# Hints on the back edges of the attention loops, a wait ahead of the mask chain, and a new order at the block boundary of the expert stage

## What is computed

```python
xn = layernorm(x)
# attention, 16 heads of 16 features
q = (xn @ Wq.T + bq) * SCALE;  k = xn @ Wk.T + bk;  v = xn @ Wv.T + bv
att = softmax(q @ k.T) @ v @ Wo.T + bo
# experts: 16, each takes the S/2 tokens of each batch with the highest route
scores = softmax(xn @ wg + bg);  mask = one_hot(top_k(scores, 2)).sum(-2)
route = scores * mask / ((scores * mask).sum(0) + EPS_GATE) * 4
seq_ids = top_k(route per expert, S // 2)
h = gelu(xn[seq_ids] @ w1 + b1);  z = xn;  z[seq_ids] += h @ w2 + b2
ffn = layernorm(z) * gamma + beta
out = x + att + ffn
```

## Time and profile before

| | us |
| --- | --- |
| median of 3 runs | 3733.28 |
| lowest and highest | 3726.79, 3736.49 |
| the profiled execution | 3726.04 |
| its span, first to last instruction | 3724.30 |
| `attend` in it, first to last matmul | 257.2 to 3160.9 |
| `finish` in it, from its first matmul | 3187.8 to 3724.3 |

### The profile page before, as it was taken

One profiled execution on the slowest core, in us unless ns is written; L12 is line 12 of the kernel. 1 busy time (PEld: TensorE's weight loads), 2 busy tenths in 40 slices (PEclk: granted clock), 3 DMA queues, 4 the chain that ended last, 5 costly groups with the idle time before them and its releaser, 6 DMA issues. The chain is left out here.

```text
span 3724.3 us, 69317 instructions
## 1 busy us (share of the span) xinstructions
PE 3461.2 (93%) x19888; PEld 1687.1 (45%) x19888; DVE 2971.2 (80%) x2989; ACT 2481.7 (67%) x4783; POOL 926.3 (25%) x1306
## 2 busy tenths in 40 slices
PE   7869999999999999999999999999999999688887
PEld 6424443443443443443434434434434442577776
DVE  7428888888887887888888888888878881578777
ACT  3534777777777777777777777777777774333332
POOL 2640111111221211111111111111212210355555
PEclk9977999999999999999999999999999995799999
DMA  3661111111111111111111111111111110322222
GB/s 100 202 184 34 45 41 41 41 46 41 50 45 40 45 41 41 41 45 40 47 47 43 44 41 41 41 41 47 48 38 48 45 32 10 99 88 81 82 85 76
DMA packets 101400, 213.01 MB, mean 57 GB/s; under 512 B 11393, under 2 KB 59585, under 8 KB 88833
## 3 DMA queue, kind: packets, MB, share of 16 engines
q1 hardware_dynamic: 98576, 207.68, 18.4%
q10 hardware_dynamic: 2544, 1.62, 0.2%
HBM read 148.42 MB, written 59.77 MB: 56 GB/s over the span
## 5 line engine op out<-in xcount | busy, mean ns | idle before, releaser
L791 DVE TENSOR_REDUCE half_max<-m_ps 128x1 f32<-128x1024 f32 x2048 | 2414.0, 1219 | 497.8 <-PE m_ps L709 488.9
L656 ACT ACTIVATE prob<-s_ps 128x512 f32<-128x512 f32 x4096 | 2132.0, 602 | 688.2 <-PE s_ps L725 670.0
L725 PE MATMUL s_ps<-q_feat,k_feat 50*128 50x512 f32 x4096 | 1528.9, 455 | 38.1 <-issue 30.5
L709 PE MATMUL m_ps<-k_feat,q_feat 48*128 48x512 f32 x4096 | 1381.7, 453 | 40.3 <-DMA k_feat<-k_parts 29.3
L725 PEld LDWEIGHTS s_ps<-q_feat,k_feat 50*128 50x128 f32 x4096 | 698.9, 189 | 1294.3 <-ACT prob L656 1094.9
L734 PE MATMUL a_ps<-prob,v_head 128*32 128x512 f32 x8192 | 1130.4, 625 | 31.5 <-issue 31.5
L709 PEld LDWEIGHTS m_ps<-k_feat,q_feat 48*128 48x128 f32 x4096 | 635.6, 191 | 144.8 <-DVE half_max L791 62.6
L549 POOL TENSOR_TENSOR shift<-row_max,shift 128x16 fp32r<-128x16 f32 x64 | 18.0, 281 | 1363.7 <-ACT shift L661 1363.7
L734 PEld LDWEIGHTS a_ps<-prob,v_head 128*32 128x32 f32 x8192 | 165.1, 109 | 287.2 <-issue 229.8
L1074 ACT ACTIVATE g_hi<-g 128x512 fp32r<-128x512 f32 x128 | 80.9, 632 | 257.1 <-DVE g L1115 256.1
L1247 POOL TENSOR_TENSOR g_lo<-g,g_hi 128x512 fp32r<-128x512 f32 x128 | 183.9, 1437 | 218.1 <-ACT g_hi L1074 218.1
(11 more groups left out here) (141 smaller groups left out, 2114.7 us busy)
## 6 DMA issues: line engine op xcount, KB each, us to landing
q_feat<-q_parts SPq DMA_DIRECT2D x128, 256.0 KB
k_feat<-k_parts SPq DMA_DIRECT2D x128, 256.0 KB
q_parts<-parts SPq DMA_DIRECT2D x32, 512.0 KB, 4.8
k_parts<-parts SPq DMA_DIRECT2D x32, 512.0 KB, 4.8
q_feat<-q_parts SPq DMA_DIRECT2D x128, 128.0 KB
k_feat<-k_parts SPq DMA_DIRECT2D x128, 128.0 KB
att_dram<-att SPq DMA_DIRECT2D x64, 256.0 KB, 15.9
mask_bc<-mask_b SPq DMA_DIRECT2D x128, 128.0 KB, 3.3
```

Of the source, the lines that this page charges most:

```text
L656: act.activation(prob[tile(r, kt) % R][:, qb * BLK:(qb + 1) * BLK], s_ps[slot(r, kt, qb, turn) % R][:, :], ACT.Exp).then_inc(exped, 1)
L709: ins = pe.matmul(m_ps[p % 2][:, k * BLK:(k + 1) * BLK], q_feat[r % 2][LOW, qt * P:(qt + 1) * P], k_feat[r % 2][LOW, key:key + BLK], start ...
L725: pe.matmul(s_ps[slot(r, kt, qb, turn) % R][:, :], k_feat[r % 2][UP, kt * P:(kt + 1) * P], q_feat[r % 2][UP, qb * BLK:(qb + 1) * BLK], sta ...
L791: dve.tensor_reduce(half_max[r][:, p // 2, p % 2:p % 2 + 1], m_ps[p % 2][:, :], AX.X, ALU.max).then_inc(maxed, 1)
```

## The change

Three edits. In `attend` all five loops get `hint_back_edge=True`. In `attend` DVE waits for the last head's `split_shift` before the mask chain. In `finish` PE's `project` moves ahead of the first `unhide` of a block, and DVE's addition of the shift (`shift_x`) moves from the end of a block to behind the statistics in the next one.

```diff
-            with pool.Fori(0, ROUNDS) as i:
+            with nc.Fori(0, ROUNDS, engines=[ENGINE.Pool], hint_back_edge=True) as i:
...
-            with sp.Fori(0, ROUNDS) as i:
+            with nc.Fori(0, ROUNDS, engines=[ENGINE.SP], hint_back_edge=True) as i:
...
-            with act.Fori(0, ROUNDS) as i:
+            with nc.Fori(0, ROUNDS, engines=[ENGINE.Activation], hint_back_edge=True) as i:
...
-            with pe.Fori(0, ROUNDS) as i:
+            with nc.Fori(0, ROUNDS, engines=[ENGINE.PE], hint_back_edge=True) as i:
...
-            with dve.Fori(1, HEADS // R) as i:
+            with nc.Fori(1, HEADS // R, engines=[ENGINE.DVE], hint_back_edge=True) as i:
...
             dve.wait_ge(search, (TOP + 1) * BIT - 1)
+            dve.wait_ge(shift_done, HEADS)
             dve.wait_ge(v_ready, HEADS)
...
-                    unhide(blk, u, e)
                     if last and e == 0:
                         project(blk - 1)
+                    unhide(blk, u, e)
...
                 ins.then_inc(renormed, 1)
+
+            def shift_x(blk):
                 dve.wait_ge(renormed, blk + 1)
-
                 dve.tensor_tensor(x_in[:, :, :], x_in[:, :, :], shift_bc[:, :].unsqueeze(1).broadcast_to([P, TPB, D]),
                                   ALU.add).then_inc(shifted, 1)
...
             def add_sum(blk):
+                dve.wait_ge(renormed, blk + 1)
                 for k in range(TPB):
...
                         add_sum(blk - 1)
                         statistics(blk - 1)
+                        shift_x(blk - 1)
```

More of the change, by code:

```diff
@@ L31 @@
 ds = bass.ds
+ENGINE = mybir.EngineType
 P = 128
@@ L1216, in _ @@
             statistics(NBLK - 1)
+            shift_x(NBLK - 1)
             scale(NBLK - 1)
```

## The result

| | before | after |
| --- | --- | --- |
| median (lowest to highest) of 4 runs each, us | 3734.89 (3726.79 to 3737.26) | 3624.80 (3613.66 to 3637.90) |
| the profiled execution; its span | 3726.04; 3724.30 | 3633.97; 3632.2 |
| granted clock over the span | 0.947 | 0.969 |

The granted clock is that of TensorE, as a share of its full speed. The ratio is 0.971, with an interval of 0.967 to 0.975: 110 us less between the medians, 92.1 between the two spans. The page after, first part, answers rows 1; the second line is the clock in tenths over 40 slices of the span, where the 6 is the last head.

The account below looks back on a forecast made before the run. PE, busy 93% of the span, was taken as the bound, losing time in stops and at low clock. Gains of 73.4 + 3.7 + 8 = 85.1 us off 3726.04 gave 3641 us, range 3606 to 3664.

Parts of the forecast that it names:

- both engines must be freed: At the attention loop's back edges, PE and ACT both lose instruction fetch time, ACT's loss ending last; hinting both gains 73.4 us.
- The 0.43 us for a hinted edge: Cost assumed for each hinted back edge in attend, taken from DVE's short-bodied loop; nine make 3.9 us.
- the 8.6: Price in us of each unhinted back edge in attend, from transpose distances; nine cost 77.3 us.
- Rival 3: Back edges in attend: the hint does nothing, only 3.7 + 8 us come, 3715 us; chance 0.07.
- Rival 2: Back edges in attend: only one of the two engines profits, half the price stays, 3678 us; chance 0.07.
- rival 4: A case in which the kernel is not faster, given a chance of 0.04; its details are not in the text.
- The mask wait: At the last head's shift, PE's stop goes because DVE now waits before the mask chain; gain 3.7 us.
- No way back up: In the last head, a fallen clock does not recover, as 77 us at 0.50 with PE full show.
- rival 1: Last head of attend: the clock stays up throughout, gaining 27 us more, 3614 us; chance 0.39.
- `finish`: At its block boundaries, PE's waits only move and split; the clock falls less often, gaining 8 us of a possible 12.9.
- the lock: In finish, POOL's num_lo holds DVE's neighbouring operation; shortening over 20 us would say it does not catch the gate.
- then the shift takes its free 1.22: In finish, after statistics 1.1 us earlier, the moved shift takes 1.22 us, leaving gate 2 unmoved within 0.1.

## Why the prediction came out

**What bounds the kernel, and both engines must be freed: right.** That ACT's stop ends last was read from rows 3, and the runs with one hint show it: nothing for PE alone, 15 us for ACT alone. The gain at the nine edges was 73.6 against 73.4 predicted.

**That the two numbers agree so closely is luck.** The 0.43 us for a hinted edge were taken from DVE's row, and 0.41 came, but these are the 0.4 us of DVE's own edge, which stands in the same head. The sum had set it down as nothing ("DVE's edges hold nobody up") and had counted it in the 8.6. The kind of head that takes 43.04 us is the one with DVE's edge alone. So of the 8.6 us some 8.2 were PE's and ACT's, all of it went, and DVE's 0.4 stayed. Hints on DVE don't take it away. The reason given for the 0.43, a jump whose target is at hand, no run shows: what the runs show is PE's branch at 0.36 us in place of 3.63 and heads that take no longer than those with DVE's edge alone.

**Rival 3, the hint does nothing: wrong.** With it the stops would stay; PE's "issue" went from ten to one. What the hint fetches, and when, no row shows. Rival 2 did not come either, nor did rival 4 (a chance of 0.04), which has the kernel slower than before: no extra stop appears inside a round.

**The exit: missed.** The sum had no term for it. It costs 4.1 us in the profiled execution and up to 8.7 in others, and only where ACT is hinted.

**The mask wait: right in size, and its clock left to a rival.** The stop gave 3.5 of 3.7 us, and POOL's subtraction (L550) takes 0.22 us, as it was to show. The forecast put the fall of the clock near the last head's start. In the profiled execution it came 15 us in and cost 7.7 us less than before; with the wait alone the clock stayed up to the end. "No way back up" fits both traces: the clock stayed at 0.50 for 57.3 us with PE busy for 57.22 of them, as it had for 77 us before. My argument for the fall, that this head has the least work, fits the run with added matmuls and is not shown by it: with the same work the clock fell in one trace and stayed up in another. What decides between them stays open. The median, 3624.8, lies between the forecast's 3641 and rival 1's 3614, since the executions differ; no single case of the prediction describes it, and with one more execution of either kind it would have moved by some 9 us. The profiled execution's 3634 is nearer to the forecast, with the clock falling 15 us later than forecast.

**`finish`: direction right, the size too small.** It gave 14.5 us in the profiled execution and 21 (12 to 24) in the median of the run with these edits alone, against 8; blocks were to take 31.2 to 31.8 and take 30.83. The bound named for being wrong, 20, was passed by that median and not by either profiled execution. But the reason attached to it, that the lock does not catch the gate, is not it. The boundary in the kernel after, which answers rows 8 and 9:

```profile
3304.25 2.43 POOL L1269 TENSOR_TENSOR num_lo<-num,num_hi 128x1024 fp32r<-128x1024 f32 x1
...
3304.38 2.85 DVE L1117 TENSOR_TENSOR g<-g,mask_bc 128x512 f32<-128x512 f32 x1
...
3308.51 1.31 DVE L1117 TENSOR_TENSOR g<-g,mask_bc 128x512 f32<-128x512 f32 x1 [1.28 <-ACT g L1073]
...
L1128 DVE TENSOR_TENSOR xe_in<-xe_in,shift_bc x16: 1190/1192/1196, 3157.3 to 3618.3; 128x1024 f32<-128x1024 f32 x16
```

The gate takes 2.85 us in place of 0.68, beside `num_lo`, and ends 0.55 us after it; the shift takes 1.19 in place of 3.28. So what is called the lock is in the rows this much: the operation of DVE that starts 0.1 to 0.2 us behind `num_lo` takes some 2.1 us more than elsewhere and ends behind it, and it caught the gate as it had caught the shift. Two lines of the kernel before which did not stand among the rows, its second gate and DVE's wait for the reciprocal deviation:

```profile
3392.54 1.28 DVE L1115 TENSOR_TENSOR g<-g,mask_bc 128x512 f32<-128x512 f32 x1 [1.27 <-ACT g L1071]
...
DVE z L1146 <- POOL rstd_z L1253: 20.3, 16, 1.6
```

From the start of `num_lo` to the second gate it was 3392.54 - 3387.15 = 5.39 us and is 4.26: 1.1 earlier, as the prediction had it.

The step that failed is "then the shift takes its free 1.22, and gate 2 with all that follows stands where it stood, within 0.1". The shift does not lie on the path: DVE waited 1.3 us a block (20.3 in 16 times) for POOL's `rstd_z` right there, and the shift fills that wait. What it costs is the 0.8 us that POOL's two operations take more. 1.1 - 0.8 = 0.3 us a block is the 30.83 in place of the best 31.16, 5 us in 15 blocks. The clock gave the other part: 0.86 us a block was there to be had, 12.9 in all, 8 were taken, and one block of 15 still falls (32.36), so 11.4. In the last block the same stretch takes 3.99 us from the statistics to the scaling, 1.61 before, and `finish` ends 2.0 later than its blocks say. The 8 us that the range of the prediction sets down as lost in `finish` no run shows: the kernels with one of the moves or both gained 8, 18 and 21 us.

**The sum.** For the profiled execution 85.1 us were predicted and 92.1 came: 73.6 + 3.5 + 14.5 from the three terms and 7.7 from the last head's clock, less 4.1 at the exit and some 3 in small pieces elsewhere. So the sum is near because what it missed cancels in part: 6.5 more in `finish` and 7.7 from the clock, against the exit and the small pieces. The median is another 9 below it; the two times near 3615 make that.

## What to carry to other kernels

Where two engines each stop at the same place, read both stops before pricing either: freeing one of them can bring nothing, even the longer one only a small part, here 15 us of 71. A stop's price must be taken from the distance of two marks in the program, since the clock behind it more than doubled it here (PE's stops of 2.6 to 3.1 us cost 7.0 each with ACT hinted). And where a second loop jumps in the same places, take the heads in which it jumps alone as the measure. Before an operation is said to lengthen a path at its new place, look for the engine's own idle time at that place, and for what its neighbour engine does there.

## What the runs showed of the hardware that was not expected

- The hinted back edges add nothing measurable on PE (3,072 matmuls and weight loads in the body of its loop) and ACT: all nine heads with them take 43.07 to 43.10 us, as those with DVE's edge alone do. Unhinted, in the trace of the kernel before, PE stopped for 2.7 to 3.2 us and ACT for 5.6 to 6.2, and a second packet came on PE's instruction queue 3.2 to 4.4 us after the first. A head with DVE's edge alone takes 43.04 us without its hint and 43.08 with it, against 42.67 without an edge.
- A loop with a hint on ACT costs once, at its end, a stop of ACT of 3.4 to 4.6 us and 4.1 to 8.7 us in all (46.80 to 51.35 us for the head in seven traces, against 42.67); PE's hint alone has no such cost (one trace, 42.67 or 42.68).
- PE's clock does not follow from how long PE is busy: 57.22 of 57.30 us at 0.50 in the changed kernel, 43.69 of 48 at 1.00 in the one with the wait alone. Once at 0.50 in the last head it stayed there, for 77 us before and 57.3 after. Behind the same hole (PE busy for 2.65 of 3.40 us), with the same program, it fell in one trace and stayed up in another. With matmuls without use beside it, it stood at 1.00 (49 us), and the median of four was 13 us lower.
- POOL's operation on 4 columns takes 1.00 us when DVE's addition of two SBUF tensors of 1024 columns has 0.9 us to go, and 0.47 when a gate of 512 has 0.4 to go; in both it ends 0.1 us after DVE's.
